# Expert loop of a two-layer macaron block: TensorE and VectorE take the slot tiles between the two activated tiles of a pair

## What is computed

```
x = x + 0.5 * moe(layernorm(x))          # before and behind the first attention
# moe: 16 experts, top 2 per row, HIDDEN 256, D_FF 512
logits = x @ router_w
top_vals, top_ids = top_k(logits, 2);  probs = softmax(top_vals)
for e in range(16):
    h = silu(x @ W1[e]) @ W2[e]
    out = out + combine[:, e:e+1] * h
```

## Time and profile before

| What | Value |
|---|---|
| Time, median of three runs | 2251.79 us |
| The three runs | 2263.23, 2251.69, 2251.79 us |
| The profiled execution, span from first to last instruction | 2250.1 us |
| TensorE matmul busy | 2000.6 us (89%) |
| VectorE busy | 1299.5 us (58%) |
| ScalarE busy | 786.1 us (35%) |
| GpSimd busy | 865.4 us (38%) |

### The profile page before, as it was taken

The page is one execution under the profiler, slowest core; times in us unless marked ns, Lnnn a source line. Parts: engine busy times, 40 slices in busy tenths (PEclk is TensorE's granted clock), DMA queues, the critical chain, the costliest instruction groups (busy, mean ns, idle before and its releaser), DMA issues. The chain is left out here.

```text
span 2250.1 us, 29291 instructions
## 1 busy us (share of the span) xinstructions
PE 2000.6 (89%) x8700; PEld 1242.8 (55%) x8701; DVE 1299.5 (58%) x2970; ACT 786.1 (35%) x1293; POOL 865.4 (38%) x684
## 2 busy tenths in 40 slices
PE   5899868888888799967599999999899999999987
PEld 5566635545554666646455555555565555555456
DVE  7322275777775722237466666666656666666525
ACT  1122244555555122213223333333413343433323
POOL 0344401231112044422036555556425555565631
PEclk9999969999999599989589999999999999999999
DMA  9111132232220811132321122122122222221101
GB/s 380 47 63 59 54 122 29 41 45 29 29 29 1 346 56 58 64 103 109 80 62 47 41 57 50 38 54 56 24 61 57 57 52 56 56 47 39 31 0 50
DMA packets 60568, 150.62 MB, mean 67 GB/s; under 512 B 12976, under 2 KB 18304, under 8 KB 58176
## 3 DMA queue, kind: packets, MB, share of 16 engines
q1 hardware_dynamic: 50208, 120.43, 20.4%
q0 software_dynamic: 9120, 24.92, 3.6%
q10 hardware_dynamic: 1152, 4.19, 0.5%
HBM read 68.95 MB, written 18.61 MB: 39 GB/s over the span
## 5 line engine op out<-in xcount | busy, mean ns | idle before, releaser
L1831 POOL TENSOR_TENSOR mla_PS<-mla_PS,mla_PT 128x1024 f32<-128x1024 f32 x192 | 457.5, 2383 | 223.2 <-ACT mla_PT L2110 220.6
L2253 DVE TENSOR_REDUCE mla_MXP<-PS 128x1 f32<-128x512 f32 x512 | 343.4, 689 | 242.5 <-PE PS L1910 236.9
L2110 ACT ACTIVATE mla_PT<-PS 128x1024 f32<-128x1024 f32 x256 | 262.5, 1026 | 402.1 <-PE PS L1929 399.5
L1938 PE MATMUL PS<-mla_PT,mla_CN 128*64 128x512 f32 x1024 | 275.3, 616 | 0.1
L1910 PE MATMUL PS<-mla_KH,mla_QH 113*128 113x512 f32 x512 | 216.2, 458 | 31.4 <-DMA mla_KL<-mla_SL 20.1
L521 DVE COPY moe_HT<-PS 128x512 f32<-128x512 f32 x92 | 63.7, 692 | 306.7 <-PE PS L644 300.9
L1929 PE MATMUL PS<-mla_QH,mla_KH 113*128 113x512 f32 x512 | 211.1, 412 | 1.0 <-ACT mla_QH L2097 1.0
L675 POOL DMA_INDIRECT moe_XS<-rows_in,moe_GI x96 | 93.5, 974 | 307.2 <-PE PS L630 171.6
L1929 PE MATMUL PS<-mla_QL,mla_KH 113*128 113x512 f32 x512 | 202.0, 395 | 0.0
L1929 PE MATMUL PS<-mla_QH,mla_KL 113*128 113x512 f32 x512 | 201.0, 392 | 0.0
L1910 PEld LDWEIGHTS PS<-mla_KH,mla_QH 113*128 113x128 f32 x512 | 90.7, 193 | 193.3 <-DVE mla_MXP L2253 123.6
(11 more groups left out here) (297 smaller groups left out, 3196.5 us busy)
## 6 DMA issues: line engine op xcount, KB each, us to landing
W<-in_W_dram SPq DMA_DIRECT2D x16, 2048.0 KB, 28.0
mla_QH<-mla_SH SPq DMA_DIRECT2D x64, 128.0 KB, 2.4
mla_KH<-mla_SH SPq DMA_DIRECT2D x64, 128.0 KB, 2.4
mla_QL<-mla_SL SPq DMA_DIRECT2D x64, 128.0 KB, 2.5
mla_KL<-mla_SL SPq DMA_DIRECT2D x64, 128.0 KB, 2.4
mla_KH<-mla_SH SPq DMA_DIRECT2D x64, 96.0 KB, 2.4
mla_KL<-mla_SL SPq DMA_DIRECT2D x64, 96.0 KB, 2.4
sums_Y<-rows_out SPq DMA_DIRECT2D x9, 512.0 KB, 6.3
```

The costliest lines, as they stand in the source:

```text
L1831: pool.tensor_tensor(PS[:, :], PT[:, slot(0), :] if k == 1 else PS[:, :], PT[:, slot(k), :], ALU.add).then_inc(s_ps.handle, 1)
L1938: ins = pe.matmul(bank(6)[h * DKVL:(h + 1) * DKVL, :], CN[:, b, k, 0:DKVL], PT[:, slot(k), h * HB:(h + 1) * HB], start=(k == 0), stop=(k = ...
L2110: act.activation(PT[:, slot(k), :], banks(st_bank(s, 0), 2)[:, :], ACT.Exp, scale=MLA_SCALE).then_inc(s_p.handle, 1)
L2253: dve.tensor_reduce(MXP[:, n // NPC, c, h, t:t + 1], bank(piece_bank(n))[:, :], AX_X, ALU.max).then_inc(s_mx.handle, 1)
```

## The change

Both edits are in the loop over pairs. TensorE issues the transposes of the first activated tile, then those of both slot tiles, then those of the second activated tile. VectorE copies in the same order: HT[0], ST[0], ST[1], HT[1]. What each operation waits for is as before.

```diff
                 with dve.Fori(0, NPAIR) as i:
-                    for u in range(2):
+                    def hidden_copy(u):
                         dve.wait_ge(s_thp.handle, s_thp.at(2 * i + u + 1))
                         dve.wait_ge(s_y.handle, s_y.at(2 * i))
                         dve.tensor_copy(HT[:, u], bank(4 + u)[:, :].rearrange("p (k s) -> p k s", s=P)).then_inc(s_thc.handle, 1)
+
+                    hidden_copy(0)
                     for u in range(2):
                         dve.wait_ge(s_tap.handle, s_tap.at(2 * i + u + 3))
                         dve.wait_ge(s_h.handle, s_h.at(2 * i + u + 1))
                         dve.tensor_copy(ST[:, u], bank(u)[:, 0:KD * P].rearrange("p (k s) -> p k s", s=P)).then_inc(s_tac.handle, 1)
+                    hidden_copy(1)
...
-                    for u in range(2):
-                        hidden_t(u, 2 * i, 2 * i + u)
+                    hidden_t(0, 2 * i, 2 * i)
                     for u in range(2):
                         slots_t(u, 2 * i + u + 2, i + 2)
+                    hidden_t(1, 2 * i, 2 * i + 1)
                     for u in range(2):
                         expert_out(u, experts[u], 2 * i, 2 * i + u)
```

## The result

The changed kernel takes 2261.77 us (median of 5 runs, 2258.05 to 2262.54); the kernel before, beside it on the same chip, 2252.0 us (median of 5, 2251.69 to 2263.23). The ratio on record is 1.0036 (the two medians alone stand 1.0043 apart), 95% interval 1.0022 to 1.005: slower by a third of a per cent, with an interval that excludes no change, and by less than the 0.5% that the prediction counted as a change. The forecast was 2264.0.

The account below looks back on a forecast made before the run. TensorE bounds the loop, its queue having hardly a margin; the later HT[1] wait costs 22 x 0.30 + 22 x 0.27 = 12.5 us, minus 0.3, so 12.2 slower than 2251.79: 2264.0 us, range 2257 to 2272.

Parts of the forecast that it names:

- What bounds a pair: In the pair loop TensorE's own row is the path; about 0.47 us a pair is lost waiting for the second Silu.
- The 0.15 that TensorE wins: At expert_out: TensorE could begin 0.44 us earlier, but HT[0]'s copy lets only 0.15 a pair be kept.
- HT[1] later by 0.45: On VectorE: HT[1], copied behind both slot copies, ends 0.45 us later, still in time for its matmuls.
- The rival in which two new hand-overs cost 0.1 each: VectorE cannot stand three copies ahead: 8.8 us on top, 2272.8 us; chance 0.10.
- extra register step on VectorE: VectorE gets one more register step beside copies that wait anyway; priced at nothing.
- The wait holds the queue: TensorE's queue stops at the wait for HT[1]; branch, expert-number loads and next hidden's addresses follow only after it.
- The rival in which the queue runs past the wait: Only TensorE decides between pairs: 46 x 0.15 = 6.9 us faster, 2244.9 us; chance 0.10.
- 0.15 of margin, 0.30 paid: Between pairs: of HT[1]'s 0.45 delay some 0.15 is margin; a pair grows 0.30 us (first stretch), 0.27 (second).
- The last hand-over of each stretch: From last pair to single tile the queue is shorter, TensorE decides: minus 0.15 us, twice.
- the border that the prediction drew (2263.1): Time where slower by 0.5% (11.3 us) begins; chances: slower 0.61, within 0.35, faster 0.04.
- The forecast gap: Ahead of hidden's first weight load: a gap of some 0.45 us, put down to issue or HT's copy.

Follow-up runs that it names:

- e1: Kernel before with only TensorE's new transpose order, VectorE copying as before: 2243.74 us, ratio 0.9957.
- e2: Kernel before with only VectorE's new copy order, TensorE as before: 2287.94 us, ratio 1.0144.
- e6: Kernel before with a third, unused load of an expert number and its check in each pair: 2273.82 us in one run.
- e9: Changed kernel without the range assertions on the two expert numbers, still loaded one by one: 2242.17 us, ratio 0.9955.
- e4: Changed kernel with both expert numbers of a pair loaded by one load instead of two: 2255.51 us, ratio 1.0012.
- e5: Kernel before with both expert numbers of a pair loaded by one load instead of two: 2252.64 us in one run.

## Why the prediction was right

**What bounds a pair** was read rightly: the second tile's transposes waited for Silu, and the wait vanishes with the new order (34.0 us over 92 waits are gone; the 4.4 over 4 at the single tiles stay).

**The 0.15 that TensorE wins** is 0.16 by the last matmul of expert_out in the trace after, and 0.16 a pair in e1, where it is kept.

**HT[1] later by 0.45**: 0.44, without a gap in front (2.24 to 2.68 behind the first transposes). The rival in which two new hand-overs cost 0.1 each falls with that. The prediction's extra register step on VectorE is not there: the trace after has one step of VectorE's queue less per pair, 46 in all; priced at nothing, it changes no sum.

**The wait holds the queue.** The 2.6 us from the wait to the last address step stayed 2.6. The rival in which the queue runs past the wait, the one on the faster side, falls by e2 (+32.6 us though no matmul waited for the copy) and by e6 and e9 (queue longer or shorter, nothing else moved). Its price was right even so: it gave 6.9 us of gain, and e1, in which the wait does not move, gained 6.6 in the stretches. By the Trainium skill, Advanced Engine Details and Errata, section Sequencer Loop, an engine's instruction is pushed into a queue and waits for its semaphores there. The wait for HT[1] sits on a register step of TensorE's queue, so it is no test of that. What bears on it is the weight load of the first activated tile, which waits for Silu: in all 46 pairs of the kernel before, the queue's next step (the earlier trace rows is one) started 0.06 us behind the end of that Silu. So here the queue's steps did not run past a waiting load either, and the trace speaks against the rival's use of the rule.

**0.15 of margin, 0.30 paid.** The pairs after the first of each stretch grew by 0.29 in the first stretch and 0.26 in the second, against 0.30 and 0.27. The sum treated all 22 hand-overs alike. From hidden to hidden the first grew by 0.63 and 0.47, but 0.29 of either lies ahead of the first transposes, in the matmuls that start 0.85 apart, which the change does not touch. From transposes to transposes the first pair grew by 0.44 in the first stretch, nearly the whole delay of HT[1] there (0.46), since it was bound by the queue already and had no margin (the load right behind its step), and by 0.28 in the second, like the others. The last hand-over of each stretch shrank by 0.16 from transposes to transposes (7.80 to 7.64), as forecast; from hidden to hidden it shows only 0.06, because hidden's first matmul is shown a tenth too early in all pairs with a wait (at 251.51, 0.01 behind its load, where the earlier trace rows have 0.11). In all the two stretches took 6.66 + 5.83 = 12.5 us more, and 11.9 from their first transposes on, where 12.2 was the forecast.

**From the stretches to the whole.** Here a term was missing. The sum let everything outside the loop stand. In the traced run the second stretch ended 12.6 us late and the kernel 10.7. The difference came back in the adapter stage, which the change does not touch. Its windows, in the columns of the earlier trace rows, before and after:

```profile
1009.29:1072.67 63.38, 47.96 (x272) 39.62 (x273) 50.06 (x206) 24.92 (x67) 14.76 (x20) 0.88 0.30 112
```

```profile
1021.60:1081.78 60.18, 45.10 (x273) 36.64 (x273) 50.82 (x206) 24.68 (x67) 14.82 (x20) 0.95 0.31 119
```

The same work took 3.2 us less at a granted clock of 0.95 in place of 0.88; later stages lost 1.6. The stage took between 61.5 and 63.8 us in the other kernels, whatever their loops did, so I take this for a variation from run to run and not for an effect of the change; that was not tested. The medians differ by 9.8, and where the other runs, which left no trace, won their 2 to 3 us is open. The forecast itself lay near the border that the prediction drew (2263.1), and those few microseconds put the time below it: what came true is not the larger chance (0.61, slower by more than 0.5%) but the one of 0.35, within it, though the interval shows a small loss. The loop's sum was right by its parts; that the whole came out within 2.2 us of 2264.0 is in part luck, since nothing in the prediction bounds what the adapter stage gives or takes.

**The forecast gap.** It stands where it was expected, ahead of hidden, and is put down to issue. Its size needs care. From the last start in expert_out to hidden's first are 0.55 to 0.60 in the first stretch, behind its first pair, against 0.216 between matmuls before; with the tenth by which hidden is shown early, 0.45 is lost, the 0.16 that TensorE won plus the 0.29 by which the pair grew. The timeline alone shows 0.18.

## What to carry to other kernels

On TensorE's queue here, a wait held up every step behind it, register loads and address steps included (e2: 0.88 us of delay, 0.73 paid a pair). So before a copy is moved later, find the step that waits for it and add up what the queue must still do before the engine's next block, even if the data are in time by far. A queue that is nearly as long as the engine's work shows no wait in the matmul row; its margin is found by the time from the last address step to the load that it serves, and a gap in the matmul row that is put down to "issue" is the sign that the margin is gone. Where that is so, loads of numbers (e4, e6) and range assertions (e9) cost as much time as matmuls would, and shortening them can decide between a gain and a loss by the same reordering (e9 against the kernel after: 8.51 against 8.95 a pair).

## What the runs showed of the hardware

A load of two numbers into TensorE's registers took 537 ns in the median (e4, e5) where a load of one took 299, so merging two loads saved 0.06 us and not one load; the very first of a kernel took 729 (e4) and 497 (before).

A range assertion, written as an argument of the load, cost TensorE's queue an address step of 151 to 156 ns and an assertion of 18, some 0.29 us with the gaps (after against e9): as much as the load itself. In the kernel after, two of them were more than the whole change could win.

TensorE's busy time went up by 13.9 us in the pairs of the two stretches while it did the same matmuls there. In the first stretch, at the same granted clock (1.00 before and after):

```profile
75.00:281.00 206.00, 200.13 (x830) 132.01 (x829) 44.86 (x92) 44.60 (x92) 88.33 (x90) 1.00 0.18 57
```

200.13 us for 830 matmuls, where the earlier trace rows had 193.21 for 830. TensorE, waiting for its own queue, looked busier, at 97% in both: the busy time counts part of the wait.
